# First layer's last batch: denominators summed and inverted on the chip's own tiles; the recurrent stage's first inputs start without the state

## The reference

```
x = x + L0(x, cond)   # attention, 8 heads of 32: softmax over keys, then @ Wo.T
x = x + L1(x, cond)   # causal convolution with 16 taps, cond as the kernel
x = x + L2(cond, x)   # GRU over 256 time steps, 16 rows of 512, state from cond
x = x + L3(x, cond)   # attention, 16 heads of 16
```

## Time and profile before

| what | us |
|---|---|
| median of 3 runs | 2847.83 |
| lowest, highest | 2840.78, 2853.43 |
| the profiled execution's own time | 2837.42 |
| its span, first to last instruction | 2835.6 |
| busy in the span: PE, DVE, ACT, POOL | 2601.0, 2114.8, 1340.7, 883.2 |
| mean granted TensorE clock | 0.973 of full |

### The profile page before, as it was taken

The page is one execution under the profiler, slowest core; times in us unless marked ns, Lnnn a source line. Parts: engine busy times, 40 slices in busy tenths (PEclk is TensorE's granted clock), DMA queues, the critical chain, the costliest instruction groups (busy, mean ns, idle before and its releaser), DMA issues. The chain is left out here.

```text
span 2835.6 us, 113854 instructions
## 1 busy us (share of the span) xinstructions
PE 2601.0 (92%) x46640; PEld 1476.2 (52%) x46640; DVE 2114.8 (75%) x4262; ACT 1340.7 (47%) x2346; POOL 883.2 (31%) x838
## 2 busy tenths in 40 slices
PE   6999999999779999999999999995999999999987
PEld 2233333333269998988888989981222222222221
DVE  4666667666768888888888888755777777777775
ACT  1555555555322222222222222221778788888877
POOL 0444444444412221112111111112234434444343
PEclk7999999999789999999999999997999999999999
DMA  1311101101100000000000000003434444444532
GB/s 43 116 49 33 53 29 51 53 27 43 28 21 0 0 1 1 0 0 0 0 0 0 0 1 0 0 1 84 97 92 107 120 98 114 117 97 114 120 91 54
DMA packets 121516, 131.65 MB, mean 46 GB/s; under 512 B 32224, under 2 KB 85368, under 8 KB 121362
## 3 DMA queue, kind: packets, MB, share of 16 engines
q1 hardware_dynamic: 115630, 123.70, 16.9%
q10 hardware_dynamic: 5760, 6.56, 0.9%
HBM read 85.83 MB, written 44.34 MB: 46 GB/s over the span
## 5 line engine op out<-in xcount | busy, mean ns | idle before, releaser
L873 PE MATMUL exp_ps<-region,gru_hT 128*16 128x128 f32 x16384 | 498.5, 274 | 44.7 <-DVE gru_hT L1000 14.0
L1544 DVE TENSOR_REDUCE x<-exp_ps 128x2 f32<-128x1024 f32 x352 | 426.3, 1222 | 103.5 <-PE exp_ps L1650 102.0
L873 PEld LDWEIGHTS exp_ps<-region,gru_hT 128*16 128x16 f32 x16384 | 428.3, 103 | 113.1 <-DVE gru_hT L1000 113.1
L402 POOL TENSOR_TENSOR l_probs<-l_probs 128x1024 f32<-128x1024 f32 x128 | 311.4, 2447 | 321.3 <-ACT l_probs L478 225.1
L1470 ACT ACTIVATE region<-exp_ps,x 128x1024 f32<-128x1024 f32 x336 | 370.2, 1110 | 79.0 <-PE exp_ps L1623 79.0
L804 POOL TENSOR_TENSOR xT<-xT,gru_hT 128x64 f32 (+1 forms) x256 | 120.0, 469 | 889.6 <-DVE gru_hT L1000 881.0
L918 ACT ACTIVATE gru_r<-exp_ps 128x128 f32<-128x128 f32 x256 | 71.0, 277 | 582.9 <-PE exp_ps L873 582.9
L958 DVE SCALAR_TENSOR_TENSOR xT<-x,condT,xT (+1 forms) x420 | 318.5, 800 | 0.1
L575 DVE TENSOR_REDUCE l_maxes<-exp_ps 128x2 f32<-128x1024 f32 x176 | 214.7, 1222 | 131.5 <-PE exp_ps L641 129.2
L858 PE MATMUL exp_ps<-region,gru_x_st 128*32 128x128 f32 x8192 | 271.7, 274 | 12.9 <-POOL gru_hT L825 12.9
L1636 PE MATMUL bank<-region,x 128*17 128x512 f32 x2048 | 272.0, 603 | 6.7 <-ACT region L1470 3.6
(11 more groups left out here) (176 smaller groups left out, 4077.7 us busy)
## 6 DMA issues: line engine op xcount, KB each, us to landing
region<-key_query_scratch SPq DMA_DIRECT2D x128, 192.0 KB
key_query_scratch<-x SPq DMA_DIRECT2D x48, 256.0 KB, 2.4
key_query_scratch<-region SPq DMA_DIRECT2D x48, 256.0 KB, 2.6
region<-in_x SPq DMA_DIRECT2D x16, 512.0 KB, 4.4
l_rden<-rden_scratch SPq DMA_DIRECT2D x128, 64.0 KB, 2.0
l_xres<-in_x SPq DMA_DIRECT2D x16, 512.0 KB, 3.7
x_scratch<-x SPq DMA_DIRECT2D x16, 512.0 KB, 2.8
l_rden<-rden_scratch SPq DMA_DIRECT2D x240, 32.0 KB, 1.8
```

The costliest lines, as they stand in the source:

```text
L402: pool.tensor_tensor(probs[:, first, :, :], probs[:, first, :, :], probs[:, second, :, :], ALU.add).then_inc(added, 1)
L873: last = pe.matmul(out[QW * j:QW * j + rows, cols], hT[:, p, k, state], group_of(wh[:, k, gate, :], j), start=False, stop=True, skip_group ...
L1544: dve.tensor_reduce(maxes[:, half, qt, head % HH:head % HH + 2], pairs[ring.place[2 * slot + 1]][:, :, :], AX_X, ALU.max).then_inc(taken[" ...
```

## The change

For batch 15 alone the denominators take another way. POOL adds no tiles. PE multiplies every tile of exponentials with the ones (two segments at each of the four places, so twice the matmuls). DVE inverts the PSUM bank, all 128 partitions, into `den_sb` (`invert_last`), and multiplies the sums by it (`scale_last`). In DVE's program the first group is inverted at slot 10 of step 15 and scaled at slot 13; the second is inverted and scaled at slot 2 of step 16, ahead of the 10 early taps with numbers 54 to 63. ACT's two copies of the denominators and SP's stores and loads for batch 15 are gone, and in step 16 SP only loads `xres`, once `out` of batch 14 is done.

In the recurrent part PE waits for `hT` behind its first 96 input records and not ahead of them.

```diff
@@ sync: step
+                if isinstance(s, int) and s > LAST:
+                    wait(sp, ready["out"], s - 1)
+                    sp.dma_start(xres[:, :, :], g.x[s - 1:s].rearrange("o (c p) t -> p (o c) t", c=CC)).then_inc(xres_loaded, 16)
+                    return
...
-                if active(s, 0):
+                if active(s, 0) and not (isinstance(s, int) and s == LAST):
                     store_den(0, n(2, 1))
@@ scalar: step
-                    if slot == 2 and active(s, -1):
+                    if slot == 2 and active(s, -1) and not (isinstance(s, int) and s > LAST):
                         evac_den(s - 1, 1)
...
-                    if slot == AT["sums"] and active(s, 0):
+                    if slot == AT["sums"] and active(s, 0) and not (isinstance(s, int) and s == LAST):
                         evac_den(s, 0)
@@ vector
+            def invert_last(grp):
+                dve.wait_ge(d_done, SEGS // 2 * LAST + 2 * (grp + 1))
+                dve.wait_ge(den_stored, 16 * 2 * LAST)
+                wait(dve, ctx_ready, 2 * LAST + grp if grp else 0)
+                dve.reciprocal(den_sb[:, :], d_ps[:, :]).then_inc(d_taken, 1)
+
+            def scale_last(grp):
+                dve.wait_ge(d_taken, 2 * LAST + grp + 1)
+                dve.wait_ge(o_taken, 2 * LAST + grp + 1)
+                dve.tensor_tensor(ctx_sb[:, LAST % 2, grp, :], ctx_sb[:, LAST % 2, grp, :], den_sb[:, :], ALU.mult).then_inc(ctx_ready, 1)
...
+                    if isinstance(s, int) and (s, slot) in ((LAST, 10), (LAST + 1, 2)):
+                        invert_last(s - LAST)
+                    if isinstance(s, int) and (s, slot) in ((LAST, 13), (LAST + 1, 2)):
+                        scale_last(s - LAST)
+                    if isinstance(s, int) and s > LAST:
+                        conv_early(SLOTS * (s - LAST) + slot)
+                        continue
@@ tensor: denominators
-                wait(pe, added, SEGS * s + 2 * n + 2)
                 if n % 2 == 0:
                     wait(pe, d_taken, 2 * s + grp)
...
+                if isinstance(s, int) and s == LAST:
+                    wait(pe, taken["st"], 16 * s + 4 * n + 4)
+                    for seg in (2 * n, 2 * n + 1):
+                        for j in range(GH):
+                            last = pe.matmul(d_ps[QW * j:QW * j + QW, :], ones[:, :], probs[:, 2 * (seg % 4) + j // 2, j % 2, :],
+                                             start=(seg % 4 == 0), stop=(seg % 4 == 3))
+                else:
+                    wait(pe, added, SEGS * s + 2 * n + 2)
...
@@ recurrent part, tensor
             pe.wait_ge(g.gru_w_loaded, 16 * 2 * TC * GATES)
-            pe.wait_ge(hT0_ready, 2)
...
             for gate in range(GATES):
                 feed(0, 0, gate, range(TC))
+            pe.wait_ge(hT0_ready, 2)
             loop(pe, step)
```

More of the change, by code:

```diff
@@ L666, in denominators @@
                 grp = n // 2
-                wait(pe, added, SEGS * s + 2 * n + 2)
                 if n % 2 == 0:
                     wait(pe, d_taken, 2 * s + grp)
-                for j in range(GH):
-                    last = pe.matmul(d_ps[QW * j:QW * j + QW, :], ones[:, :], probs[:, 2 * (2 * n % 4) + j // 2, j % 2, :],
-                                     start=(n % 2 == 0), stop=(n % 2 == 1))
+                if isinstance(s, int) and s == LAST:
[6 more added lines that the diff above has]
+                    wait(pe, added, SEGS * s + 2 * n + 2)
+                    for j in range(GH):
+                        last = pe.matmul(d_ps[QW * j:QW * j + QW, :], ones[:, :], probs[:, 2 * (2 * n % 4) + j // 2, j % 2, :],
+                                         start=(n % 2 == 0), stop=(n % 2 == 1))
                 last.then_inc(d_done, 1)
```

## The result

The changed kernel is slower: a median of 2867.03 us over 4 runs (2864.66 to 2870.74), beside 2844.93 us over 4 runs of the kernel before on the same chip. The ratio is 1.0077, with a 95% interval of 1.0056 to 1.0098: 22 us more where I had forecast 10 less. The profiled execution took 2865.15 us, with a span of 2863.4 us (before: 2837.42 and 2835.6).

A forecast was written before the change was run, and what follows sets the result against it. In the touched stretch PE and its clock bound, except 13.81 us from denominators to projection, mostly DMA latency. 11.8 - 4.7 + 1.8 + 0.8 = 9.7 us gained, from median 2847.83 to 2838.1; range 2827 to 2847.

The forecast's parts named there:

- The step that failed: Outside steps 15 and 16 and the recurrent stage's first microseconds (95.8 us), nothing changes except through the clock.
- The round trip: Batch 15's last denominators skip DRAM: projection starts at 771.89 instead of 783.66, 11.8 us gained.
- cover forecast: Step 16: ten late taps stay hidden beside the projection and ACT's copy, with 1.6 us to spare.
- The doubled products: Step 15, slots 5, 9, 13: PE's denominator matmuls double, costing 1.93 + 1.06 + 1.93 less 0.22, 4.7 us.
- 1.8 us of clock gain: Step 15: denser work ends both low-clock stretches 2 us earlier each, gaining 1.8 us.
- the case that the prediction had set beside its own: Step 15's low stretches: extra matmuls change nothing as PE is already 99 to 100% busy; gain 1.8 us smaller.
- rival 2: Step 15: doubled products bring the full clock back at once, 15.5 us gained, about 2832; chance 12%.
- The recurrent start: PE's first input records start 1.5 us sooner, low clock may eat nearly all; 0.8 us gain taken.
- rival 1: Clock stays at 0.50 from 721 until the last denominators: 3 to 4.6 us slower, about 2851; chance 8%.
- rival 4: Step 16: the `xres` load is late, needing over 7 us, each us beyond costing one; chance 2%.
- rival 3: Recurrent part gives nothing, PE's start held otherwise or clock eating it: 8.9 us gained, about 2839; chance 20%.
- the signs: Low clock fills step 15, projection waits for `xres`, or DVE's ten taps end behind ACT's last copy.

The follow-up runs named there:

- ACT +4: Changed kernel with 4 more instructions (8 met waits) in ACT's stream, SP's left as changed: ratio 1.0082, median 2867.08 us.
- SP +7: Changed kernel with 7 more instructions (12 met waits) in SP's stream: 2829.65 us in one run.
- POOL +16: Changed kernel with 14 more instructions in SP's stream and 16 more in POOL's: 2825.23 us in one run.
- PE +196: Changed kernel with 14 more instructions in SP's stream and 196 more in PE's: 2830.95 us in one run.
- experiment 7: Changed kernel with 14 more SP instructions, plus POOL's, PE's or DVE's stream lengthened by 16, 196 or 125: recurrent stage 1110.6, 1111.0, 1106.9 us.
- experiment 1: Changed kernel with 14 more instructions (26 met waits) in SP's stream, its last loop back in its old place: ratio 0.9943, median 2830.20 us.
- experiment 2: Kernel before the change with 114 more instructions (226 met waits) in SP's stream: ratio 1.0116, median 2876.76 us.

## Why the prediction was wrong, point by point

**The step that failed** is in its first part: "The rest (2835.6 less 95.8 us) it cannot alter except through the clock." I left the last stage out of the sum because no line of it changes. The change altered it through the place of SP's instructions. Shown by runs: 14 do-nothing instructions cure it (-37.0 us), it can be brought about in the code before (+30.8 and +39.3 us), six places agree with one rule, two of them forecast by it, and the other engines' places don't matter for it. Read from the trace, in one pass: three fetches inside SP's pause, the pause 5.5 us longer, DVE's wait of 6.52 (before 1.50), PE's of 5.37, then 6.8 us of low clock. The 38.6 us over five passes are 7.7 us for each (the passes themselves are 7.2 us longer, 112.6 against 105.4, which is 36 us; the rest lies around them). Of a pass the low clock is up to 6.8 x 0.45 = 3.1 us, in four of the five, and the pause behind SP would be the rest; this split is an estimate. Argued only: that four blocks don't fit where three do. Why five blocks are fetched in a pass when the loop touches four, and three of them in the pause, is open.

Of the fetches the Trainium skill ("Runtime: NRT & Kernel Launch", "Instruction fetch mechanics") says that a taken branch to a target outside the window that the engine holds forces a fetch before execution goes on. The traces agree in kind: the extra packets come in every pass of the loop, three of five while SP stands still at its turn. They differ in the grain: the page speaks of blocks of 256 instructions, the runs fit 128 and exclude 256 for this queue. I had not weighed this rule, and it was the one that spoke against the change.

**The round trip: right.** Timeline of all engines, after; it answers to the earlier trace rows and, for the reciprocal.

```profile
763.98 1.06 PE L684 MATMUL bank<-l_probs,l_v 128*32 128x512 f32 x8
764.08 0.40 SPq L344 DMA_DIRECT2D l_xres<-in_x  x1
...
764.86 1.90 PE L698 MATMUL bank<-l_probs,l_ones 128*32 128x512 f32 x16
...
766.83 3.36 DVE L577 RECIPROCAL l_den<-bank 128x512 f32<-128x512 f32 x1 [5.14 <-PE bank L698]
770.22 0.69 DVE L582 TENSOR_TENSOR l_ctx<-l_ctx,l_den 128x512 f32<-128x512 f32 x1
770.83 6.04 DVE L561 SCALAR_TENSOR_TENSOR region<-x,condT,region 128x448 f32<-128x448 f32 x10
...
771.01 2.04 PE L737 MATMUL bank<-l_wo,l_ctx 128*128 128x256 f32 x4 [4.25 <-DVE l_ctx L582]
...
778.45 1.02 ACT L511 ACTIVATE x<-bank 128x1024 f32<-128x1024 f32 x1 [12.74 <-PE bank L739]
```

Last sums to projection: 7.03 us, forecast 7.44, before 19.21. The handover came out at 4.25 us, as summed. Of the 0.4 us one half is that the sixteen records took 1.90 us where I had put 2.12, the other that they started 0.88 us behind the sums and not 1.07. Reciprocal and multiplication are on their rows to the hundredth. `xres` was issued at 764.08 and held nobody; the ten taps ended at 776.87, 2.60 us ahead of the end of ACT's copy (cover forecast: 1.6, with taps of 0.67 us; they took 0.60). The projection took 7.4 us at 0.61 (forecast 7.3).

**The doubled products: mis-sized.** PE's timeline, after, beside the earlier trace rows:

```profile
723.99 3.64 PE L698 MATMUL bank<-l_probs,l_ones 128*32 128x512 f32 x16
...
739.28 3.56 PE L698 MATMUL bank<-l_probs,l_ones 128*32 128x512 f32 x16
...
752.38 3.64 PE L698 MATMUL bank<-l_probs,l_ones 128*32 128x512 f32 x16
```

All three ran at the low clock, the second too, which I had put at full clock (+1.06): low stretches of 23.9 and 6.8 us, 30.7 in all, against the 30.6 of the earlier trace rows (13.6 and 17.0). So my 1.8 us of clock gain did not come in this execution: the low time moved and did not shrink, the case that the prediction had set beside its own. Yet first scores to last sums took 55.1 us against 53.3: +1.8, where 4.7 - 1.8 = 2.9 was forecast. The 4.7 us were too many: with the low time as long as before, the added records push other work of PE out of it, and in sum they cost what they take at the full clock, 3 x 1.06 less 0.22 = 2.96 us (an estimate from the earlier trace rows). The 1.2 us that are left stay open. Eight kernels here have the new denominators. In four of them (ACT +4, SP +7, POOL +16, PE +196) the low time was 17.0 us and the stretch 49.2 us, 4.1 less than before; 13.7 us less of it at 0.45 each is 6.2, and 55.1 - 49.2 = 5.9 agrees. That is nearly rival 2's 6.9 us, so in these four the clock gain did come, and larger than the 1.8 us. Which of the two patterns comes is not tied to any one of the paddings, and the cause is open.

**The recurrent start: right in itself, given back behind it.** PE and POOL, after, beside the earlier trace rows:

```profile
792.98 3.64 PE L889 MATMUL exp_ps<-region,gru_x_st 128*32 128x128 f32 x64 [11.37 <-POOL gru_x_st L854]
796.37 1.49 PE L889 MATMUL bank<-region,gru_x_st 128*32 128x128 f32 x32
797.67 1.93 PE L904 MATMUL exp_ps<-region,gru_hT 128*16 128x128 f32 x64
```

```profile
792.45 0.39 POOL L854 COPY gru_x_st<-region 128x128 f32<-128x128 f32 x1 [84.44 <-POOLq L243]
```

From POOL's copy to the first record with the state it is 5.22 us, before 5.98: 0.8 gained, as forecast, with the inputs at 3.64 us instead of 3.27 for the same low clock. The stage as a whole is 1.8 us longer, so some 2.6 us are lost behind its start; that this is the place of DVE's loop is my reading of experiment 7, not shown.

**The sum.** From the first scores of step 15 to the last stage the profiled execution gained 8.5 us (10.3 in the first attention less 1.8), experiment 1's 8.0, against 9.7 forecast; in ACT +4 and SP +7, 14.9 and 14.0. In the profiled execution the misses partly cancel: the round trip gave 0.4 us more, the doubled products with the clock cost 1.1 us less, and the recurrent stage gave 2.6 us less than forecast. By the runs the same terms, with the last stage left alone, were worth some 16 us (experiment 1), more than the forecast and more than these traces place. What was left out weighed four times the forecast sum. Of the rivals none had it. What rival 1 says of the clock was seen in the code before (experiment 2), rival 2 in half of the kernels, rival 4 in none; rival 3's outcome, nothing from the recurrent part as a whole, came, but not by its reasons, since PE did start earlier and 0.8 us of it stood when the state was read. None of the signs came that the prediction had named for being wrong: they too lay inside the 95.8 us. The chance of 3% for slower by over 0.5% stood for the spread of the runs alone.

**The better version.** Experiment 1's kernel beats both: 0.9943 [0.9925, 0.9962] of before. Its one-run relatives with 7 instructions on SP (2829.65 us) and with POOL's padding (2825.23 us) are not told apart from it by one run each.

## What to carry to other kernels

Before an edit that shortens or lengthens an engine's instruction stream is costed, look which loops stand behind it on that engine, and how long they are: here a loop of 321 instructions is free in three blocks of 128 and costs 7.7 us a turn in four. After an edit look at the instruction queue's packets in every stage, not only in the one edited; a stage that got slower with the same instruction counts and new fetches is cured by a few waits that are already met. And judge an edit by the stretch it touches (here from first scores to the last stage) beside the whole, or a gain of 8 us is lost under a loss of 39 in lines that nobody touched.

## What the hardware showed that I had not expected

- SP's loop of 321 instructions is fetched anew in each pass (five packets of 8 KB) at three of the six places tried, and not at the other three; the last stage then takes 31 to 39 us more than 922.
- The price grows on its way: SP's own pause was 5.5 us longer, a pass is 7.2 us longer, and in four of the five the clock fell while PE waited.
- Products that use all 128 rows and four column groups, 3.64 us long and back to back with scores, did not raise the clock in a stretch of 23.9 us in which PE was 95% busy; in other kernels the same step was low for 17.0 us in all instead of 30.7.
- POOL's additions beside DVE's taps took 17.91 us for two in experiment 2; one takes 2.33 us at best.
